# A graph kernel's last edge pass: a block's values weighed in four instructions of two edge columns, in place of one

## What is computed

```python
q = (x @ Wq + bq).reshape(n, 8, 32); k = ...; v = ...        # n = 6250 nodes, 8 heads of 32
e = (edge_attr @ We).reshape(-1, 8, 32)                      # 100000 edges, ordered by target
k_j = k[src] + e
v_j = v[src] + e
alpha = jnp.sum(q[dst] * k_j, axis=-1) / jnp.sqrt(32.0)
ex = jnp.exp(alpha - segment_max(alpha, dst)[dst])
alpha = ex / segment_sum(ex, dst)[dst]
out = segment_sum(v_j * alpha[:, :, None], dst) + x @ Ws + bs
```

## Time and profile before

| | before |
|---|---|
| median of 3 runs | 5677.88 us |
| lowest, highest | 5673.19, 5679.74 us |
| profiled execution, from its first to its last instruction | 5673.3 us |
| VectorE busy | 3824.3 us (67%) |
| GpSimd busy | 3388.4 us (60%) |
| TensorE busy, matmuls | 2860.0 us (50%) |
| L1166, the changed instruction | 98 times, 224.6 us |

### The profile page before, as it was taken

One profiled execution on the slowest core, in us unless ns is written; L12 is line 12 of the kernel. 1 busy time (PEld: TensorE's weight loads), 2 busy tenths in 40 slices (PEclk: granted clock), 3 DMA queues, 4 the chain that ended last, 5 costly groups with the idle time before them and its releaser, 6 DMA issues. The chain is left out here.

```text
span 5673.3 us, 49658 instructions
## 1 busy us (share of the span) xinstructions
PE 2860.0 (50%) x13052; PEld 2232.1 (39%) x13052; DVE 3824.3 (67%) x6117; ACT 1441.9 (25%) x2526; POOL 3388.4 (60%) x3382
## 2 busy tenths in 40 slices
PE   7513200000000000015899986888888888884777
PEld 5412200000000000014677633777776777673456
DVE  7357778786454545546543464989899998995763
ACT  1113333332233333311222211222222222221320
POOL 0267777777777777753440276777777777773200
PEclk9655555555555555556799998999999999896888
DMA  3133344432363333323232355999999999993114
GB/s 101 36 84 108 107 130 148 130 104 83 103 220 110 109 110 109 110 87 124 93 124 68 107 191 191 317 319 323 319 319 321 319 323 318 323 318 113 67 47 148
DMA packets 290231, 961.79 MB, mean 170 GB/s; under 512 B 79248, under 2 KB 119831, under 8 KB 248468
## 3 DMA queue, kind: packets, MB, share of 16 engines
q0 software_dynamic: 171296, 483.60, 28.6%
q1 hardware_dynamic: 118788, 476.59, 24.9%
HBM read 626.03 MB, written 345.69 MB: 171 GB/s over the span
## 5 line engine op out<-in xcount | busy, mean ns | idle before, releaser
L1249 PE MATMUL e_psE<-e_we,e_eaT 128*128 128x256 f32 x3136 | 903.5, 415 | 279.3 <-DVE e_wv L1148 179.3
L1111 POOL DMA_INDIRECT e_kv<-kv,rec x784 | 875.7, 1117 | 266.3 <-issue 253.7
L779 POOL DMA_INDIRECT g_g<-t,rec x784 | 777.1, 991 | 254.0 <-issue 253.7
L779 POOL DMA_INDIRECT g_g<-t,dst_of x784 | 743.6, 949 | 259.3 <-issue 257.2
L1249 PEld LDWEIGHTS e_psE<-e_we,e_eaT 128*128 128x128 f32 x3136 | 649.4, 210 | 400.7 <-ACT e_eaT L1192 299.4
L1407 PE MATMUL j_psM<-ident,tail 128*128 128x128 f32 x32 | 7.2, 416 | 1149.0 <-PEq L53 1149.0
L1250 PE MATMUL e_psE<-e_kv,ident 128*128 128x256 f32 x1568 | 509.8, 409 | 0.0
L816 DVE TENSOR_TENSOR_SCAN g_wv<-g_fx,g_wv 128x2176 f32<-128x2176 f32 x98 | 459.0, 4684 | 0.2 <-issue 0.2
L1407 PEld LDWEIGHTS j_psM<-ident,tail 128*128 128x128 f32 x32 | 6.8, 322 | 1149.8 <-issue 1149.8
L1118 POOL DMA_INDIRECT e_q<-q,q_of x392 | 370.9, 946 | 119.7 <-issue 119.7
L956 ACT ACTIVATE g_st<-g_wv 128x2048 f32<-128x2048 f32 x98 | 375.9, 3836 | 0.0
(11 more groups left out here) (519 smaller groups left out, 6620.8 us busy)
## 6 DMA issues: line engine op xcount, KB each, us to landing
state<-e_st SPq DMA_DIRECT2D x98, 1088.0 KB, 6.2
e_ea<-in_edge_attr SPq DMA_DIRECT2D x98, 896.0 KB, 9.8
state_f<-g_st SPq DMA_DIRECT2D x49, 1088.0 KB, 4.4
state_b<-g_st SPq DMA_DIRECT2D x49, 1088.0 KB, 4.3
m_work<-xs SPq DMA_DIRECT2D x119, 128.0 KB, 2.3
ys<-m_work SPq DMA_DIRECT2D x119, 128.0 KB, 1.7
xs<-g_ta SPq DMA_DIRECT2D x28, 512.0 KB
g_g<-t,rec POOLq DMA_INDIRECT x784
```

Of the source, the lines that this page charges most:

```text
L779: pool.indirect_dma_start(g[:, u, j, :], None, tab, bass.IndirectOffsetOnAxis(ap=at_, axis=0)).then_inc(gat[u], 16)
L1111: pool.indirect_dma_start(kv[:, u, b, :], None, c.kv, bass.IndirectOffsetOnAxis(ap=c.rec[:, t, 1:2], axis=0)).then_inc(gkv[u][b // 4], 16)
L1249: nc.tensor.matmul(half, eaT[:, m, j, k, :], we[:, k, :], start=(k == 0), stop=False)
```

## The change

L1166 becomes a loop, written out by Python, of four tensor_tensor instructions. Each takes two of the block's eight edge columns (128x512 elements) of `wv` and the two matching columns of the factors `cw`. The wait for `cwd` ahead of the first and everything behind the last stay as they were.

```diff
                     v.wait_ge(cwd, blk + 1)
-                    weighed = wv[:].rearrange("p b (h k) -> p b h k", k=C)
-                    tt(weighed, weighed, cw[:, :, 1:B1].rearrange("p h b -> p b h").unsqueeze(3).to_broadcast([P, B, H, C]),
-                       ALU.mult)
+                    quarter = B // 4
+                    for part in range(4):
+                        weighed = wv[:, part * quarter:(part + 1) * quarter, :].rearrange("p b (h k) -> p b h k", k=C)
+                        factors = cw[:, :, 1 + part * quarter:1 + (part + 1) * quarter]
+                        tt(weighed, weighed, factors.rearrange("p h b -> p b h").unsqueeze(3).to_broadcast([P, quarter, H, C]),
+                           ALU.mult)
                     tt(by_head(before[:]), by_head(st[:, 1 - u, B - 1, 0:D]), of_head(0), ALU.mult)
                     v.drain()
```

## The result

| | before | changed |
|---|---|---|
| median | 5677.71 us | 5684.33 us |
| runs, lowest to highest | 21, 5668.87 to 5683.38 | 21, 5679.97 to 5690.57 |
| changed / before | | 1.0014, interval 1.0008 to 1.0021 |
| profiled execution, span | 5673.3 us | 5688.9 us |
| first to last L1140, 97 blocks | 1610.0 us | 1617.2 us |

The account below looks back on a forecast made before the run. VectorE's own instruction sequence in the last edge pass was taken as the bound, 16.57 us a block. 98 blocks x 0.228 us gave + 22.3 us, other terms taken as 0: median 5700.2 us, range 5690 to 5711.

Parts of the forecast that it names:

- VectorE sets the pace, GpSimd's shorter stalls give nothing by themselves: Last edge pass: VectorE's own sequence sets 16.57 us a block; gathers some 0.6 us a block shorter save no time.
- The rival with GpSimd's pace: Edge pass: GpSimd sets the block's length and its stalls shrink 0.6 us a block, 59 us faster; chance 0.04.
- Fixed part 0.076 us, 0.228 us a block: Weighing L1166: each of three added instructions a block costs a fixed 0.076 us, together 0.228 us, 22.3 us in all.
- The lower rows that I had (L847, 0.05): Two 128x512 instructions of L847, one input in PSUM, gave the lowest fixed part found, 0.05 us an instruction.
- Seams cost VectorE nothing: Gathers slipping in between the weighing's parts cost 0, bound 12 us; the rival of costly seams, + 34 us, had 0.12.
- All of it is on the path: VectorE's queue in the edge pass: nothing behind the weighing or the pass absorbs the added 0.228 us a block.
- Below nothing: ... 4 us: Accumulating steps L1176 lose 4 us to gathers; with other phases some of that might go; taken as 0.
- +-0.1 us a block, 9 us at most: VectorE's instruction supply: six more instructions in the loop's body may add or hide an issue gap; taken as 0.
- The issue gap: A gap of 0.19 us for "issue" on VectorE in every second block of the edge pass, read as instruction supply.
- Within the noise: Rival: fixed part of 0.05 us (14.4 us), less 6 us of gather and supply disturbances, + 8 us; chance 0.08.
- The Trainium skill's rule that the pair of ports is kept for a whole instruction: VectorE and GpSimd share SBUF ports, kept by whoever starts first; as a rival, gathers delay parts, + 115 us, chance 0.01.

Follow-up runs that it names:

- the last two kernels compared: Kernel before with L1140 as tensor_reduce and one instruction ahead of the loop, 5665.56 us; changed kernel with L1140 as tensor_reduce, 5683.34 us.

## Why the prediction was wrong

- *VectorE sets the pace, GpSimd's shorter stalls give nothing by themselves*: right. The changed kernel has no steady wait of VectorE for a gather, and GpSimd waits in 94 blocks. The shorter stalls gave 0.04 us a pair, at the scan. The rival with GpSimd's pace is out.
- *Fixed part 0.076 us, 0.228 us a block*: the term was right in kind and 10% high. At the seams of the four parts it is 0.069 us (0.602 from start to start), + 0.206. The lower rows that I had (L847, 0.05) were the wrong ones to trust, the pairs of the earlier trace rows the right ones.
- *Seams cost VectorE nothing*: nearly. Between the parts nothing; L1168 behind them takes 0.04 us more in each block, 4 us in all, since a gather now arrives there. I had taken 0 with a bound of 12.
- *All of it is on the path*: right, by the last two kernels compared. That their 22.1 us are the forecast's 22.3 is partly luck: the weighing alone gives 98 x 0.206 = 20.2, and L1168 and the scan make up the rest.
- *"Below nothing: ... 4 us" and "+-0.1 us a block, 9 us at most"*: here the prediction failed, in the second term, the one for the instruction supply. It let the change give back at most some 13 us in both and took 0 for both. Given back were 0.24 + 0.12 + 0.04 us in two blocks, 49 x 0.40 = 19.6 us. The gap's own 0.12 us, 6 us in all, are within that term's bound. The copy's 0.24, 12 us, hang on the same gap and were not in my list at all; the one added instruction ahead of the loop brought both back, 17.1 us, without the change. The copy's 0.41 us stood in the earlier trace rows as its last line but one. I read that block for gaps between instructions, and this wait is inside an instruction's length: the waits of the earlier trace rows don't show it. The question that I did not put to the row is why eight elements take 0.41 us there and 0.17 elsewhere.
- *The issue gap* I had noticed, and I wrote that six more instructions may hide it. They did, in full: it went from a step to the drain behind L1173. The prediction should have counted which instruction it would fall on.
- *"Within the noise"*, at 0.08, named + 8 us and is the nearest in time, but with the wrong parts: a fixed part of 0.05 where it is 0.07, and 6 us of relief where there were 19.6, less 5 of new disturbance.
- *The Trainium skill's rule that the pair of ports is kept for a whole instruction*: I set it aside because no step of L1176 was delayed by more than 0.06. That was right for L1176's steps and wrong for a copy. The Trainium skill, "SBUF — State Buffer", section "Who interferes with whom", makes just this difference: a copy can run in a mode that takes both ports and then contends with GpSimd, a reduce never does. The pair of runs with copy and reduce agrees, 0.41 against 0.17 us; but the copy is held only in the later part of a gather, not from its start.

## What to carry to other kernels

Before pricing an edit on a full engine, look at the spread of every instruction's duration on it (least, median, most, mean): a mean of 288 ns with a least of 166 is a wait that no list of waits has, and an edit that moves it by a tenth of a us may remove it. Where GpSimd issues indirect DMAs all the time, a tiny fp32 copy on VectorE can cost more in waiting (0.24 us) than in work (0.17); a one-element tensor_reduce did the same work unheld and was worth 0.2% here. A gain or loss of a few tenths of a per cent from an edit in a hardware loop should be checked against an edit that only shifts the program by one instruction: here one added instruction, without any use, gave 0.24%, and a second one took it back.

## What was not expected of the hardware

- A gather in flight holds a copy of 128x8 fp32 until its own end, if the copy starts 0.52 to 0.71 us into the gather's 0.95, and not at 0.48 or before. A tensor_reduce of the same elements at the same place takes 0.17 us.
- Whether the gather or a step of 0.48 us goes first turns on less than 0.1 us: with the gather 0.07 us behind the step's start the gather is unstretched and the step takes 0.53, with 0.15 us the step is unstretched and the gather takes 1.14.
- A stall of 0.12 us at one place of a hardware loop of 80 instructions, which moves one instruction earlier when one is added ahead of the loop, and which only shows where nothing else delays that instruction.
